# A recurrent attention layer with a routed expert layer on one core: normalising shared anew, and the second batch's k, v, r products spread over every second pair

## The reference, cut to what matters

```python
xn = layernorm(x)
xs = xn shifted by one token
xm = xn * time_mix + xs * (1 - time_mix)
k, v, r = exp(min(xm @ Wk.T, 60)), xm @ Wv.T, xm @ Wr.T
wkv, sum_k = decayed sums over time of k*v and of k     # per head, one decay rate each
s = (sigmoid(r) * wkv / (sum_k + 1e-16)) @ Wo.T
e = argmax(xn @ Wg + bg)                                # one of 8 experts per token
y = relu(xn @ W1[e] + b1[e]) @ W2[e] + b2[e]            # 128 -> 512 -> 128
out = x + s * silu(y)
```

## Time and profile before

| what | value |
|---|---|
| time, median of 3 runs | 176.46 us (175.15 to 176.85) |
| time of the profiled execution | 175.93 us |
| its span, first to last instruction | 174.1 us |
| lies around the span | 1.83 us |
| busy: TensorE, weight loads, VectorE | 149.5, 119.0, 122.8 us |
| busy: ScalarE, GpSimd | 102.4, 98.5 us |
| mean granted TensorE clock | 0.963 |

### The profile page before, as it was taken

One profiled execution on the slowest core, in us unless ns is written; L12 is line 12 of the kernel. 1 busy time (PEld: TensorE's weight loads), 2 busy tenths in 40 slices (PEclk: granted clock), 3 DMA queues, 4 the chain that ended last, 5 costly groups with the idle time before them and its releaser, 6 DMA issues.

```text
span 174.1 us, 3350 instructions
## 1 busy us (share of the span) xinstructions
PE 149.5 (86%) x954; PEld 119.0 (68%) x954; DVE 122.8 (71%) x262; ACT 102.4 (59%) x295; POOL 98.5 (57%) x149
## 2 busy tenths in 40 slices
PE   7995899996797689995999794985999999999960
PEld 2433465442575477874789693885999999999960
DVE  2498994999999999999999999999600000000971
ACT  2946975976484366564782922744886677642720
POOL 7879920017777475764455876746564464460550
PEclk9999999999699969999699999999999999999997
DMA  4943999706354142342323631543645552115973
GB/s 80 318 155 136 386 295 341 292 3 210 106 166 124 34 161 90 109 168 85 111 86 116 211 105 49 171 147 105 230 153 178 175 178 96 45 45 184 361 297 120
DMA packets 15808, 27.96 MB, mean 161 GB/s; under 512 B 2952, under 2 KB 3520, under 8 KB 15792
## 3 DMA queue, kind: packets, MB, share of 16 engines
q1 hardware_dynamic: 12944, 23.10, 37.7%
q0 software_dynamic: 2272, 4.66, 9.5%
q10 hardware_dynamic: 576, 0.01, 0.2%
HBM read 10.78 MB, written 6.75 MB: 101 GB/s over the span
## 4 chain that ended last, share of the span: by engine, by line
PE 66%; issue 7%; ACT 6%; DMA 5%; POOL 4%; DVE 4%; another core or an unknown queue 3%; ACTq 2%; DVEq 0%
PE ps L1064 21%; PE ps L1047 20%; PE ps L1079 9%; PE ps L989 7%; DMA wg<-in_L_ffn_Wg 3%; PE ps L948 3%; DMA xg<-xn_rows,gidx 2%; PE ps L1038 2%; PE ps L939 2%; PE ps L1059 1%; ACT ohhi_hidif L857 1%; POOL ser L441 1%; DVE ohlo L607 1%; ACT kT L875 1%
## 5 line engine op out<-in xcount | busy, mean ns | idle before, releaser
L467 POOL DMA_INDIRECT g_rows<-gout,sidx x39 | 40.1, 1028 | 25.4 <-ACT gout L866 18.6
L460 POOL DMA_INDIRECT xg<-xn_rows,gidx x32 | 34.0, 1064 | 33.3 <-DVE gidx L658 15.8
L1047 PE MATMUL ps<-xn_sb,w1e 128*128 x312 | 43.7, 282 | 3.8 <-issue 3.7
L1047 PEld LDWEIGHTS ps<-xn_sb,w1e 128*128 128x128 f32 x312 | 39.9, 198 | 4.6 <-issue 4.6
L857 ACT ACTIVATE ohhi_hidif<-ps,b1T 128x128 f32<-128x128 f32 x104 | 30.2, 384 | 19.1 <-PE ps L1047 16.9
L1064 PE MATMUL ps<-w,ohhi_hidif 128*128 x208 | 29.6, 282 | 2.5 <-issue 2.5
L748 DVE TENSOR_TENSOR kT<-ps,kT 128x512 f32<-128x512 f32 x8 | 5.3, 688 | 37.3 <-ACT kT L917 36.4
L989 PE MATMUL ps<-xmT,wT 128*128 128x512 f32 x48 | 25.7, 649 | 4.5 <-ACT rT L877 1.9
L1064 PEld LDWEIGHTS ps<-w,ohhi_hidif 128*128 128x128 f32 x208 | 25.6, 192 | 5.6 <-issue 5.3
L866 ACT COPY gout<-ps 128x128 f32<-128x128 f32 x39 | 11.1, 284 | 15.7 <-remote 10.1
L857 ACT ACTIVATE hidT<-ps,b1T 128x128 f32<-128x128 f32 x52 | 15.0, 380 | 8.3 <-remote 4.2
(11 more groups left out here) (165 smaller groups left out, 220.1 us busy)
## 6 DMA issues: line engine op xcount, KB each, us to landing
w1e<-w SPq DMA_DIRECT2D x39, 256.0 KB
x_sb<-in_L_attn_x SPq DMA_DIRECT2D x8, 256.0 KB, 6.1
w<-in_L_ffn_W SPq DMA_DIRECT2D x1, 2048.0 KB, 9.5
xn_rows<-xn_sb SPq DMA_DIRECT2D x2, 1024.0 KB, 12.4
kT<-g_rows SPq DMA_DIRECT2D x8, 256.0 KB, 4.4
out_x<-kT SPq DMA_DIRECT2D x8, 256.0 KB, 2.1
g_rows<-gout,sidx POOLq DMA_INDIRECT x39
xg<-xn_rows,gidx POOLq DMA_INDIRECT x32
```

Of the source, the lines that this page charges most:

```text
L460: g.indirect_dma_start(xg[j][:, :], None, xn_rows, bass.IndirectOffsetOnAxis(gidx[:, s:s + 1], 0)).then_inc(gathered[j], 16)
L467: g.indirect_dma_start(g_rows, bass.IndirectOffsetOnAxis(sidx[:, s:s + 1], 0), gout[j][:, :], None).then_inc(scattered[j], 16)
L1047: last = t.matmul(psH[n % DEEP][:, cols], w1e[n % W1_RING][:, cols], xgT[:, bass.ds(held.of(n), 1), :].rearrange("p o t -> p (o t)"), star ...
```

## The change

- Normalising: GpSimd does it before the decay rates, takes tiles 0 and 1 in batch 0 and tile 0 in batch 1; VectorE takes tile 3 of the first two blocks, none of the next two, and tiles 1 and 3 in batch 1; ScalarE tile 2, and tiles 2 and 3 of blocks 2 and 3. The splitting of b2 goes from VectorE to GpSimd. ScalarE's order of copies in the head changes, and the weights for k, v, r are turned round first of all instead of last.
- The load of w2 is issued after the stores of `xn_rows`, and TensorE waits for it at slot 2.
- `INV_AFTER` goes from 8 to 10.
- The first register loads of TensorE come before `transpose_rows(0)` instead of after it.
- Batch 1's products are ordered block by block (k, v, r of a block), and `kvr(12 + m)` runs in slot 2m (`FILL_AT`), so they end in slot 22 instead of slot 11. Keys are capped one block at a time, the exps of batch 1 stand in slots 9, 15, 20 and 24, and `Y_BANK` has two banks up to slot 25.
- Register addresses of w2 and of the bias are `e` times a fixed size, with the chunk as a fixed offset.
- `rw[q]` is written tile by tile, so that the stationary operand of the projection is contiguous.

```diff
-INV_AFTER = 2 * NBB
+TANH_AFTER = 2 * NBB
+INV_AFTER = TANH_AFTER + 2
 EARLY = 3 * NBB
 LATE = BATCH * 3 * NBB - EARLY
-EXP_AFTER = 9
+FILL_AT = {2 * m: EARLY + m for m in range(LATE)}
+FILL_END = 2 * LATE
+EXP_AT = {9: NBB, 15: NBB + 1, 20: NBB + 2, 24: NBB + 3}
+CAP_BEFORE = {1: NBB, 3: NBB + 1, 4: NBB + 2, 5: NBB + 3}
 WARM_UP = 46
 TAYLOR = 9
+POOL_TILES = [(0, 1)] * NBB + [(0,)] * NBB
+DVE_TILES = [(3,)] * 2 + [()] * 2 + [(1, 3)] * NBB
+ACT_TILES = [(2,)] * 2 + [(2, 3)] * 2 + [(2,)] * NBB
 SMALL_DECAY = 0.5
 ROUND = 12582912.0
 HALF_STEP = 127.0 / 256.0
 BQ = E * HC
 BK = 3 * BQ
+
...
-        KVR = [(w, c) for b in range(BATCH) for w in range(3) for c in range(b * NBB, (b + 1) * NBB)]
+        KVR = ([(w, c) for w in range(3) for c in range(NBB)]
+               + [(w, c) for c in range(NBB, NB) for w in range(3)])
         AFTER_KVR = {pair: m + 1 for m, pair in enumerate(KVR)}
         bank_of = lambda m: psK[m % 3] if m < EARLY else psS
-        Y_BANK = [(psY, psT1)[n % 2] if n < LATE + 2 else (psS, psY, psT1)[n % 3] for n in range(SLOTS)]
+        Y_BANK = [(psY, psT1)[n % 2] if n < FILL_END + 2 else (psS, psY, psT1)[n % 3] for n in range(SLOTS)]
         Y_LAST = [max([m for m in range(n) if Y_BANK[m] is Y_BANK[n]], default=-1) for n in range(SLOTS)]
...
-            sp.dma_start(w2[:, :, :], W2.rearrange("e (c p) d -> p (e c) d", p=P)).then_inc(ld_w2, 16)
...
             for b in range(BATCH):
...
+            sp.dma_start(w2[:, :, :], W2.rearrange("e (c p) d -> p (e c) d", p=P)).then_inc(ld_w2, 16)
...
+            for k in range(NB):
+                if k % NBB == 0:
+                    pool.wait_ge(ln_ready, k // NBB + 1)
+                for j in POOL_TILES[k]:
+                    n = k * TPB + j
+                    g.tensor_scalar(xn_sb[:, n, :], x_sb[:, n, :], rstd[:, n:n + 1], nbias[:, n:n + 1],
+                                    ALU.mult, ALU.add).then_inc(xn_pool, 1)
...
-            def cap_keys(b):
-
-                here = slice(b * T, (b + 1) * T)
-                dve.wait_ge(kvr_out, AFTER_KVR[0, (b + 1) * NBB - 1])
+            def cap_keys(q0, q1):
+
+                here = slice(q0 * BLK, q1 * BLK)
...
+                by_tile = rw[q].rearrange("p (j r) -> p r j", j=TPB)
+                in_time = lambda t, s: t[:, s].rearrange("p (r j) -> p r j", j=TPB)
+                lower, upper = slice(0, BLK // 2), slice(BLK // 2, BLK)
+                v.scalar_tensor_tensor(out=by_tile[:, 0:P // 2, :], in0=in_time(psG[:, :], lower), scalar=0.5,
+                                       in1=in_time(rden, lower), op0=ALU.mult, op1=ALU.mult).then_inc(dve_step, 1)
+                dve.wait_ge(dve_step, n0 + RDEN_B)
+                v.scalar_tensor_tensor(out=by_tile[:, P // 2:P, :], in0=in_time(psG[:, :], upper), scalar=0.5,
+                                       in1=in_time(rden, upper), op0=ALU.mult, op1=ALU.mult)
+                dve.wait_ge(dve_step, n0 + RW_A)
                 v.scalar_tensor_tensor(out=rw[q][:, 0:1], in0=sig0[:, :], scalar=0.5,
-                                       in1=rden[:, 0:1], op0=ALU.mult, op1=ALU.mult)
-                dve.wait_ge(dve_step, n0 + RDEN_B)
-                v.scalar_tensor_tensor(out=rw[q][:, half_b], in0=num[:, BLK // 2 - 1:BLK - 1], scalar=0.5,
...
+                if q in CAP_BEFORE:
+                    cap_keys(CAP_BEFORE[q], CAP_BEFORE[q] + 1)
+                if q == 1:
+                    mix_shifted(6)
+                    mix_shifted(7)
                 dve.wait_ge(k_ready, q + 1)
...
             deviation(0)
             for k in range(NBB):
                 normalise(k)
+            deviation(1)
             copy_xnT(0)
-            deviation(1)
+            act.wait_ge(wT_ps, 1)
+            s.copy(wT[:, :, :].rearrange("p t d -> p (t d)"), psW[:, :]).then_inc(wT_ready, 1)
             copy_xnT(1)
+            normalise(4)
+            normalise(5)
+            copy_xnT(2)
+            normalise(6)
+            normalise(7)
+            copy_xnT(3)
             act.wait_ge(ld_small, 16 * 2)
             mix_here(0)
-            copy_xnT(2)
-            mix_here(1)
-            copy_xnT(3)
-            for k in range(NBB, NB):
-                normalise(k)
             act.wait_ge(ld_bg, 16 * TPB)
             copy_logits(0)
             copy_xnT(4)
+            mix_here(1)
+            copy_xnT(5)
             mix_here(2)
-            copy_xnT(5)
             copy_xnT(6)
             mix_here(3)
             copy_xnT(7)
+            copy_logits(1)
             mix_here(4)
-            copy_logits(1)
...
-                                        bias=b1T[:, bass.ds(experts.of(n) * HC + c, 1)])
+                                        bias=b1T_e[:, bass.ds(experts.of(n), 1), c:c + 1].rearrange("p o c -> p (o c)"))
...
-                if n < LATE:
-                    copy_kvr(EARLY + n)
+                if n in FILL_AT:
+                    copy_kvr(FILL_AT[n])
                 if n < NBB - 2:
                     exp_k(n + 2)
-                if EXP_AFTER <= n < EXP_AFTER + NBB:
-                    exp_k(NBB + n - EXP_AFTER)
+                if n in EXP_AT:
+                    exp_k(EXP_AT[n])
                 if n >= LAG:
...
+            pe.wait_ge(ld_proj, 16 * 4)
+            for m in range(4):
+                last = t.transpose(psW[:, m * P:(m + 1) * P], wnat[:, m, :], ident[:, :])
+            last.then_inc(wT_ps, 1)
...
-                    pe.wait_ge(kvr_out, EARLY + min(n, LATE))
+                    pe.wait_ge(kvr_out, EARLY if n < FILL_END else EARLY + LATE)
...
-                                    w2[:, bass.ds(e * HC + c, 1), :].rearrange("p o d -> p (o d)"),
+                                    w2_e[:, bass.ds(e, 1), cols].rearrange("p o d -> p (o d)"),
...
-                    last = t.matmul(S_BANK[q][:, j * P:(j + 1) * P], every(rw[q], j), wT[:, 3, :],
+                    last = t.matmul(S_BANK[q][:, j * P:(j + 1) * P], rw[q][:, j * P:(j + 1) * P], wT[:, 3, :],
...
             for m in range(INV_AFTER, EARLY):
                 kvr(m)
-            transpose_rows(0)
             pe.wait_ge(experts_ready, 1)
-            pe.wait_ge(bias_ready, 1)
-            pe.wait_ge(sel_ready, 3)
-            pe.wait_ge(ld_w2, 16)
             experts.fetch_for(0)
             pe.wait_ge(held_ready, 1)
             held.fetch_for(0)
+            transpose_rows(0)
+            pe.wait_ge(bias_ready, 1)
+            pe.wait_ge(sel_ready, 3)
             for n in range(SLOTS):
                 if n < AHEAD:
                     transpose_rows(TURN_AT[n])
                     pe.wait_ge(kvr_out, EARLY - 1 + n)
                 if n == LAG:
                     pe.wait_ge(idx_ready, 1)
+                    pe.wait_ge(ld_w2, 16)
                 layer1(n)
-                if n < LATE:
-                    kvr(EARLY + n)
+                if n in FILL_AT:
+                    kvr(FILL_AT[n])
                 if n >= LAG:
                     layer2(n - LAG)
                 if AHEAD <= n < len(TURN_AT) and TURN_AT[n]:
```

## The result

The changed kernel takes 176.68 us (median of 20 runs, 174.43 to 179.03), the kernel before 175.96 (20 runs, 173.03 to 178.36). The medians lie 0.7 us apart, 0.4%; the ratio is 1.0095, 95% interval 1.005 to 1.0139. So there is no gain but a loss of 0.4 to 1%, where I had forecast 171.5 us and given 0.71 to a gain.

The account below looks back on a forecast made before the run. TensorE's queue sets the pairs' end, 21 us above undisturbed work, with waits for copies and late signals. 0.4 - 7.9 + 3.0 + 1.0 - 0.97 = -4.5 took 175.93 to 171.5 us; range 167.0 to 177.5.

Parts of the forecast that it names:

- The products, -7.9 us: In the pairs: k, v, r products in every second pair remove 4.5 us of waits and 3.4 of lower-clock excess.
- the three waits: TensorE's stands of 1.30, 1.26 and 1.92 us before k, v, r products, each for ScalarE's copy of the product before.
- -7.9 + 3.0 + 1.0: Pairs: -7.9 for waits and slow clock, +3.0 given back for late signals, +1.0 for slots 12 to 22.
- my first rival: Late signals set the pace of the pairs wherever the products stand: 175.4 us, chance 0.20.
- -0.97 for the projection: Tail: the contiguous projection shrinks from 15 to 7.6 us, removing VectorE's 0.97 us wait for it.
- The same twelve products cost the same 10.3 us: In the pairs: moving the twelve k, v, r products to every second pair leaves their TensorE cost at 10.3 us.
- +1.0 for slots 12 to 22: Later pairs, now with products and two banks instead of three, lose 1.0 us to late signals; ends 0 and +6.
- The slower rival: Late signals in slots 12 to 25 stop TensorE until its clock falls: three stops 181.2 us, two 178.0; chance 0.10.
- Head, +0.4: Before the pairs: indices 1.5 us later, first pair at 45.3 instead of 44.92; +0.4 us, ends -0.6 and +1.5.
- Register arithmetic, 0: TensorE's sequencer: 156 fused register operations fall to at least 39, at the outside 6.4 us, counted as 0.
- the second rival: Less register work relieves the late signals in the pairs: 167.3 us, chance 0.18.
- Half clock: TensorE in the pairs: at most two stretches at half clock behind the start if the forecast is right.

Follow-up runs that it names:

- no_gather: Changed kernel without GpSimd's 32 indirect gathers, TensorE transposing tiles of x instead: 155.37 us, where the kernel before takes 175.85.
- direct_gather: Changed kernel with each indirect gather replaced by a plain transfer of 128 rows in order: 157.83 us, where the kernel before takes 175.85.
- before_spread: Kernel before with only the k, v, r products spread to every second pair, with their keys, exps and banks: 159.32 us, against 157.42 before.
- rows_unused_2: Changed kernel with gathers kept but their rows unread, TensorE transposing tiles of x without waiting: 158.30 us, against 157.22 for the kernel before.
- changed_kept_busy: Changed kernel with 12 and 3 products of ones in TensorE's waits for the first two gathered rows: 160.75 us, against 157.80 for the kernel before.

## Why the prediction was wrong, point by point

**The products, -7.9 us: the step that failed.** "Gone are the three waits, 1.30 + 1.26 + 1.92 = 4.5 us, and the excess at the lower clock behind them". The waits are gone, and the pairs last 107.6 us instead of 108.3: 0.7 us less, where -7.9 + 3.0 + 1.0 had promised 3.9. My reading of the waits was right (the row at 55.84 names "issue", but ScalarE's copy of the product before had ended just ahead of it, at 55.79); what I made of it was not. They were where TensorE's lateness surfaced, not its cause, and with the waits away it stands elsewhere, 11.1 us against 11.8. I had read that three engines are released 3.3 us late and that six us of idling come without a product in the way, and still charged 4.5 us to the coupling. That was my first rival, and for the pairs it is the one that came true; its 175.4 was still too low, since its -0.97 for the projection failed too. What makes the signals late is named by no_gather and direct_gather, the indirect gathers; how they act is open. So is what the spreading does by itself on a late chip: the 0.7 us is the sum of all parts of the change.

**"The same twelve products cost the same 10.3 us"** is true of TensorE and false of the kernel. In the second pair a product covered the wait for rows. Moved on, it leaves 2.56 us of waiting against 0.18, together with the later gathers. before_spread gives the whole price on an early chip, 1.9 us, the stand in slot 28 with it. I gave +1.0 for slots 12 to 22 and nothing for slots 1 to 3. The slower rival had its place wrong too: the clock is at 1.00 from 90 us to the end of the projection.

**Head, +0.4.** First pair forecast 45.3, measured 45.56; the indices come 1.3 us later, of the 1.5 forecast: 0.9 by the two products and 0.4 that TensorE is later already when it finishes `ranks`. The first gather is 1.85 us later (38.64 to 40.49), as GpSimd adds 0.6 that I had put at nothing. And I took the first pair as the measure, where on an early chip the third and fourth gathered tiles are late as well; waiting for rows costs the changed kernel 1.8 us there (rows_unused_2). What the later gathers cost on a late chip no run shows.

**Register arithmetic, 0.** No run isolates it, and my count was wrong: there are still 156 fused operations, only shorter (55 ns in the earlier trace rows):

```profile
L1081 PEldq FUSED_REGOPS  x156: 46/46/46, 51.6 to 152.0; - x156
```

So the second rival had no foundation. The rule of the Trainium skill (Runtime: NRT & Kernel Launch, Instruction fetch mechanics) isn't tested by this either, as nearly the same code is fetched: 8 packets of 0.13 MB in both.

**Projection.** 7.31 us, forecast 7.6. VectorE no longer waits for it and its last pair of sums starts at 168.01 instead of 169.03, 1.0 us earlier, as the 0.97 forecast had it. None of it reaches the end, since GpSimd's DRAIN ends at 173.9 us with and without the change. I read the chain and never asked what each engine does behind its last instruction.

**Half clock.** At most two stretches behind the start were forecast and the trace shows one, 64.1 to 67.6 us; but the one at the start grew from 3.4 to 6.8 us. By changed_kept_busy, on an early chip, its price is nil as long as rows are late.

## What to carry to other kernels

A wait that goes away moves the bound only if what it waited for was in time: where several engines are released late together, look for what disturbs the signals before decoupling anybody. Work that looks movable may be the cover of a wait; see what its new neighbours wait for, for each of the first few rounds and not for the first alone. Where buffers are handed out by a formula that changes over at some round, check that the two rounds at the change-over don't share one. In a tail, look at the closing rows of each engine, and let the one with the long DRAIN finish first.

## What the runs showed that I had not expected

- The same program has medians of 157.2 to 157.8 us on three chips and of 175.9 and 177.4 on two, and the difference of some 19 us goes when the 32 indirect gathers do (155.37 us on a late chip). On late chips TensorE stands between single matmuls and its signals come some 2 to 4 us late, while scatters of the same form and queue do no harm: in no_gather they all run. The records of TensorE have modelled ends; the Trainium skill (Perfetto Trace Analysis, Tensor Engine Instruction (MATMUL, LD_WEIGHTS)) says so too, and that the semaphore goes out only once PSUM has taken the bytes. The trace agrees that the two can lie apart, by 3 us at 70.95 and 73.92.
- GpSimd's closing DRAIN takes 7.57 us and starts with its last sum; behind a scatter it takes 7.74, and in no_gather, without the 32 gathers, 4.95. Why, no run shows. VectorE's takes 1.2, ScalarE's 0.67.
- Fifteen products of ones hold the clock at 1.00 through the wait for the rows, and the kernel is no faster for it: 1.9% slower than before, as without them.
